# A masked attention kernel: mask adds moved from TensorE to GpSimd, and a reordered front

## What is computed

```python
h = jnp.maximum(_layernorm(x, axis=-1), 0.0)
neib_att = jnp.tanh(neigh @ Wn1 + bn1) @ Wn2 + bn2      # (4096, 32)
value = neigh @ Wv + bv                                  # (4096, 128)
x_att = jnp.tanh(h @ Wx1 + bx1) @ Wx2 + bx2              # (4096, 32)
ws = leaky_relu(x_att @ neib_att.T, 0.01)                # (4096, 4096)
ws = softmax(where(adj > 0, ws, NEG_BIG), axis=1)
out = x + concatenate([h @ Wfx + bfx, ws @ value], axis=1)
```

## Time and profile before

| what | value |
|---|---|
| median of 3 runs | 485.35 us (484.95 to 485.37) |
| the profiled execution | 485.15 us, its span 482.8 us |
| busy, share of the span | PE 96%, PEld 88%, DVE 89%, ACT 89%, POOL 54% |
| scores of step 0 start | 31.59 us |
| scores of step 11 start | 60.93 us |
| last scores start | 446.92 us |
| granted clock of TensorE, mean | 0.998 |

### The profile page before, as it was taken

How to read it: one execution, slowest core, us unless ns; L and a number is a source line. 1 busy time by engine, 2 the same in 40 slices (tenths; PEclk the granted TensorE clock), 3 DMA queues, 4 the chain that set the end, 5 groups by cost and what they waited for, 6 DMA issues and landing times.

```text
span 482.8 us, 10844 instructions
## 1 busy us (share of the span) xinstructions
PE 464.3 (96%) x3728; PEld 424.5 (88%) x3728; DVE 427.7 (89%) x820; ACT 428.3 (89%) x714; POOL 258.4 (54%) x361
## 2 busy tenths in 40 slices
PE   8997789999999999999999999999999999999997
PEld 7975579998899899998999899999899899999896
DVE  3678899999999899989999999989999899999764
ACT  2464899999999999999999999999999999999973
POOL 3108247853677547945686557845686455454300
PEclk9999999999999999999999999999999999999999
DMA  8944635457555655557456654657457554553000
GB/s 303 304 88 90 153 67 89 81 90 163 106 88 93 130 118 100 100 90 157 93 88 109 131 110 91 109 99 159 79 95 139 91 88 79 108 100 56 11 12 12
DMA packets 32373, 51.51 MB, mean 107 GB/s; under 512 B 2368, under 2 KB 22976, under 8 KB 32320
## 3 DMA queue, kind: packets, MB, share of 16 engines
q0 software_dynamic: 9216, 33.56, 42.5%
q1 hardware_dynamic: 22816, 17.17, 11.0%
q10 hardware_dynamic: 288, 0.10, 0.2%
HBM read 80.19 MB, written 4.19 MB: 175 GB/s over the span
## 4 chain that ended last, share of the span: by engine, by line
PE 75%; ACT 5%; issue 3%; DVE 3%; POOLq 0%; POOL 0%; DVEq 0%; ACTq 0%
PE ps_turned L922 20%; PE ps_product L943 11%; PE ps_product L945 11%; PE ps_product L944 11%; PE ps_scores L900 10%; PE ps_scores L899 6%; PE ps_product L865 3%; ACT scores L561 3%; ACT pt_hi L523 2%; DVE scores L706 2%; PE ps_product L857 1%; PE ps_product L841 1%; ACT scores L549 1%; PE ps_product L848 1%; PE ps_product L954 1%
## 5 line engine op out<-in xcount | busy, mean ns | idle before, releaser
L453 POOL TENSOR_TENSOR scores<-scores,mask 128x512 f32<-128x512 f32 x117 | 136.4, 1166 | 116.9 <-ACT scores L549 116.3
L688 DVE TENSOR_TENSOR pt_lo<-ps_turned,pt_hi 128x512 fp32r<-128x512 f32 x256 | 173.9, 685 | 20.8 <-PE ps_product L945 9.8
L523 ACT ACTIVATE pt_hi<-ps_turned 128x512 fp32r<-128x512 f32 x256 | 158.1, 618 | 20.9 <-PE ps_turned L922 20.3
L943 PE MATMUL ps_product<-pt_hi,v_hi 128*128 128x256 f32 x512 | 164.9, 322 | 0.1
L922 PE MATMUL ps_turned<-ident,scores 128*128 128x128 f32 x1024 | 153.8, 273 | 0.8 <-DVE pt_lo L688 0.6
L561 ACT ACTIVATE scores<-scores,low_top 128x1024 f32<-128x1024 f32 x128 | 151.5, 1183 | 0.0
L945 PE MATMUL ps_product<-pt_lo,v_hi 128*128 128x256 f32 x512 | 144.5, 282 | 0.0
L944 PE MATMUL ps_product<-pt_hi,v_lo 128*128 128x256 f32 x512 | 144.0, 281 | 0.0
L549 ACT ACTIVATE scores<-ps_scores 128x1024 f32<-128x1024 f32 x128 | 133.3, 1041 | 9.6 <-PE ps_scores L900 9.4
L922 PEld LDWEIGHTS ps_turned<-ident,scores 128*128 128x128 f32 x1024 | 121.9, 140 | 17.7 <-issue 2.0
L706 DVE CUSTOM_DVE_ANT_0 scores<-ps_scores,scores,low_top 128x1024 f32<-128x1024 f32 x96 | 122.5, 1276 | 0.9 <-ACT scores L549 0.4
(11 more groups left out here) (70 smaller groups left out, 359.8 us busy)
## 6 DMA issues: line engine op xcount, KB each, us to landing
adj_in<-in_adj POOLq DMA_DIRECT2D x60, 512.0 KB, 5.4
scores<-in_neigh_t SPq DMA_DIRECT2D x8, 512.0 KB, 7.9
x_rows<-in_x SPq DMA_DIRECT2D x7, 512.0 KB, 5.9
x_left<-in_x SPq DMA_DIRECT2D x8, 256.0 KB, 5.7
x_right<-in_x SPq DMA_DIRECT2D x16, 128.0 KB, 5.3
scores<-in_adj POOLq DMA_DIRECT2D x4, 512.0 KB, 6.4
out_h<-x_left SPq DMA_DIRECT2D x8, 256.0 KB, 2.3
out_h<-x_right SPq DMA_DIRECT2D x16, 128.0 KB, 2.1
```

The source lines that it names most:

```text
L453: pool.tensor_tensor(half, half, mask[:, s % MASK_RING, BANK:CHUNK], ALU.add).then_inc(masked, 1)
L523: act.activation(pt_hi[:, (2 * b + u) % HI_RING], pt[:, u], ACT.Copy).then_inc(hi_done, 1)
L688: dve.tensor_tensor(pt_lo[:, u], pt[:, u], pt_hi[:, (2 * b + u) % HI_RING].bitcast(FP32), ALU.subtract).then_inc(lo_done, 1)
L943: pe.matmul(product_of(g), v_hi[:, block, :], high, start=block == 0, stop=False)
```

## The change

In the loop, from step 11 on, TensorE writes the mask of the first 256 columns alone (QUARTER = 256), with one matmul, and the scores of the first half are made by two matmuls of 256 columns. GpSimd adds the mask to the other 768. ScalarE's relu comes first in its step. VectorE's `close` comes last ahead of the mask, and x work comes before the neighbour rest. In the front, the four loads into `adj_front` are issued together, the masks of chunks 4 to 11 are made in place by four operations over two chunks each and bypass the ring, warming transposes are left out, and x's first transposes come one neighbour step earlier. Several constants of the x schedule move.

```diff
 FRONT = 4 * LOAD
-TURN_X = 4
-FILL = (6, 6, 6, 4, 0, 0, 0, 0)
+TURN_X = 3
+FILL = (6, 0, 0, 0, 0, 0, 0, 0)
 EXP_LAG = CHUNKS + 1
...
-X_LOAD = -12
-X_STATS = (-6, -6, -6, -4)
+X_LOAD = -16
+X_STATS = (-7, -6, -5, -4)
 X_AGGR = -2
 X_RSTD = (-2, -2, -1, 0)
-X_NORM = (1, 3, 3, 4)
-X_TURN = (6, 8)
+X_NORM = (3, 4, 5, 5)
+X_TURN = (6, 7)
 X_FIRST, X_TANH = 10, 10
 X_SECOND = (14, 14)
 X_STACK = (14, 14)
-X_WIDE, X_LEFT = (15, 17, 19, 19), 19
-X_LEFT_LOAD, X_SUM = 8, (13, 18)
-X_RIGHT = 14
+X_WIDE, X_LEFT = (15, 18, 19, 19), 19
+X_LEFT_LOAD, X_SUM = 10, (13, 17)
+X_RIGHT = 7
 V_START, V_STRIDE = 2, 2
 LEFT_0 = 5
-AHEAD_STATS = 0
-WIDE_0 = 1
+AHEAD_STATS = -1
+WIDE_0 = 3
+FRONT_MASKS = (1, 2, 5, 7)
 V_FRONT, V_LAG = 4, 1
 POOL_MASKS = BACK_LAG
+QUARTER = BANK // 2
 WARM_UP = 15
...
         front_ready = [sem(f"front_ready{i}") for i in range(FRONT // LOAD)]
-        mask_done = sem("mask_done")
+        mask_done, front_masked = sem("mask_done"), sem("front_masked")
         scored = sem("scored")
...
             return b // ASTEPS + 2 if b >= 0 and b % ASTEPS == 0 and b // ASTEPS < AGROUPS - 2 else None
+        def ring_place(n):
+            return n - FRONT if n >= ADJ_RING else n
+        def made_in_front(n):
+            return ADJ_RING <= n < ADJ_RING + FRONT
+        def mask_of_chunk(n):
+            return adj_front[:, n - ADJ_RING, :] if made_in_front(n) else mask[:, ring_place(n) % MASK_RING, :]
...
             pool.wait_ge(rows_in[NEIGH_GROUPS - 1], 16)
-            load_adj(2 * LOAD)
-            pool.wait_ge(x_ahead_in, 16)
-            load_adj(3 * LOAD)
+            for p in range(FRONT // LOAD):
+                load_adj(ADJ_RING + p * LOAD)
             for i in range(NEWTON + 1):
                 rstd_of(1, i)
-            load_adj(4 * LOAD)
-            load_adj(5 * LOAD)
             for i in range(TILES):
...
                 if s % LOAD == 0 and n < STEPS and not ADJ_RING <= s < ADJ_RING + FRONT:
-                    pool.wait_ge(mask_done, s + LOAD)
+                    pool.wait_ge(mask_done, ring_place(s) + LOAD)
                     load_adj(n)
...
                     pool.wait_ge(risen, s + 1)
-                    half = scores[:, parity * TILES + tile, c * CHUNK + BANK:(c + 1) * CHUNK]
-                    pool.tensor_tensor(half, half, mask[:, s % MASK_RING, BANK:CHUNK], ALU.add).then_inc(masked, 1)
+                    rest = scores[:, parity * TILES + tile, c * CHUNK + QUARTER:(c + 1) * CHUNK]
+                    pool.tensor_tensor(rest, rest, mask_of_chunk(s)[:, QUARTER:CHUNK], ALU.add).then_inc(masked, 1)
                 for i in range(NEWTON + 1):
...
                 if s == GSTEPS:
-                    act.wait_ge(mask_done, ADJ_RING + FRONT)
+                    act.wait_ge(masked, ADJ_RING + FRONT - POOL_MASKS)
                 if s == (TILES - 1) * CHUNKS:
...
             def step(s):
+                rise(s)
                 hi(s, 0)
                 aggregate(s)
-                rise(s)
                 hi(s, 1)
...
-                k = n
-                if ADJ_RING <= n < ADJ_RING + FRONT:
-                    source = adj_front[:, n - ADJ_RING, :]
-                    dve.wait_ge(front_ready[(n - ADJ_RING) // LOAD], 16)
-                else:
-                    source = adj_in[:, n % ADJ_RING, :]
-                    dve.wait_ge(adj_ready[n % ADJ_RING // LOAD], 16 * ((n - FRONT if n >= ADJ_RING else n) // ADJ_RING + 1))
-                if n >= MASK_RING:
-                    dve.wait_ge(scored, n - MASK_RING + 1)
-                if n - MASK_RING >= POOL_MASKS:
-                    dve.wait_ge(masked, n - MASK_RING + 1 - POOL_MASKS)
-                dve.tensor_scalar(mask[:, n % MASK_RING, :], source, 0.0, MASKED, ALU.is_le,
+                if made_in_front(n):
+                    return
+                r = ring_place(n)
+                dve.wait_ge(adj_ready[r % ADJ_RING // LOAD], 16 * (r // ADJ_RING + 1))
+                if r >= MASK_RING:
+                    gone = r - MASK_RING
+                    if gone >= ADJ_RING:
+                        gone += FRONT
+                    dve.wait_ge(scored, gone + 1)
+                    if gone >= POOL_MASKS:
+                        dve.wait_ge(masked, gone + 1 - POOL_MASKS)
+                dve.tensor_scalar(mask[:, r % MASK_RING, :], adj_in[:, r % ADJ_RING, :], 0.0, MASKED, ALU.is_le,
                                   ALU.mult).then_inc(mask_done, 1)
+            def front_mask(p):
+                dve.wait_ge(front_ready[p], 16)
+                pair = adj_front[:, p * LOAD:(p + 1) * LOAD, :].rearrange("p a n -> p (a n)")
+                dve.tensor_scalar(pair, pair, 0.0, MASKED, ALU.is_le, ALU.mult).then_inc(front_masked, 1)
...
             def x_work(s):
+                for p in range(FRONT // LOAD):
+                    if s == FRONT_MASKS[p]:
+                        front_mask(p)
                 if s == AHEAD_STATS:
...
                 lo(s, 0)
+                x_work(s)
+                neigh_rest(s)
+                lo(s, 1)
                 close(s)
-                neigh_rest(s)
-                x_work(s)
-                lo(s, 1)
                 if POOL_MASKS <= s < STEPS - 2:
...
                 if h == 0:
-                    pe.wait_ge(mask_done, k + 1)
+                    if made_in_front(s):
+                        pe.wait_ge(front_masked, (s - ADJ_RING) // LOAD + 1)
+                    else:
+                        pe.wait_ge(mask_done, ring_place(s) + 1)
                     if s == 0:
...
                         pe.wait_ge(x_att, s // GSTEPS + 1)
-                half = slice(h * BANK, (h + 1) * BANK)
-                on_pool = h == 1 and s >= POOL_MASKS
-                if not on_pool:
-                    pe.matmul(ps[:, s % 2, half], ident_bf16, mask[:, s % MASK_RING, half], start=True, stop=False)
-                last = pe.matmul(ps[:, s % 2, half], xs[:, parity, tile * P:(tile + 1) * P],
-                                 neib[:, c * CHUNK + h * BANK:c * CHUNK + (h + 1) * BANK], start=on_pool, stop=True)
+                attention = xs[:, parity, tile * P:(tile + 1) * P]
+                def part(first, end, masked_here):
+                    cols = slice(first, end)
+                    if masked_here:
+                        pe.matmul(ps[:, s % 2, cols], ident_bf16, mask_of_chunk(s)[:, cols], start=True, stop=False)
+                    return pe.matmul(ps[:, s % 2, cols], attention, neib[:, c * CHUNK + first:c * CHUNK + end],
+                                     start=not masked_here, stop=True)
+                if s >= POOL_MASKS and h == 0:
+                    part(QUARTER, BANK, False)
+                    last = part(0, QUARTER, True)
+                else:
+                    last = part(h * BANK, (h + 1) * BANK, s < POOL_MASKS)
                 if h == 1:
```

## The result

The changed kernel takes 493.86 us (median of 4 runs, 490.58 to 495.50) where the kernel before takes 485.15: a ratio of 1.0173, with a 95% interval of 1.0139 to 1.0206. It is slower by 1.7%. The forecast was 472.6 us, with a range of 466 to 481.

What follows compares the result with a forecast made beforehand. TensorE was taken as the first bound, tied with ScalarE in plain steps. From 485.15 us, 10.8 for the loop and 1.3 and 0.4 for the front came off, giving 472.65, stated as 472.6, range 466 to 481.

Steps and rivals of the forecast that it cites:

- TensorE's split: Loop from step 11: narrower mask and score matmuls save 0.107 us a step over 101 steps, 10.8 us.
- GpSimd's longer add: Loop: adding 768 columns instead of 512 takes 1.59 us instead of 1.166, hidden, so no cost.
- relu first: ScalarE's step: the relu ahead of both copies delays VectorE's conversion and leaky pass enough to cover the longer add.
- front: Before the loop: 1.3 us from fewer warming transposes, 0.4 from the earlier x branch; steps 0 to 11 zero, 2 either side.
- constants and VectorE's order: Loop: moved x loads, stats and VectorE's close were costed at nothing.
- the longer add is therefore covered by the reordering: Plain step: the add ends 2.73 us after the relu's start, the leaky pass comes at 2.98, so no cost.
- crowd: GpSimd, steps 3 to 6: late adds cost about 0.5 us a group, cancelled by an equal gain on the exp chain.
- Rival 3: Loop: VectorE's conversion meets a running add in every step, 16 waits a group; slower, up to 491.5 us. Chance 0.08.
- The work of steps 3 to 5: GpSimd in each group: 11.4 us of work against 9.7 of time, so step 6's add can be 1 to 2 us late.
- the forecast 0.59: Plain step on TensorE: mask and score matmuls move the stream by 0.59 us instead of 0.69.
- Rival 1: Loop: ScalarE takes over and a group's eight plain steps gain nothing; 5.4 us instead of 10.8, so 478. Chance 0.20.
- TensorE stays busy: Front: with the warming transposes removed the granted clock stays at 1.00, so no loss there.

Runs made afterwards that it cites:

- e10: e3 with TensorE's split matmuls but GpSimd's old 512-column add, so columns 256 to 511 get no mask from step 11 on: 477.43 us.
- e3: Kernel before with only ScalarE's relu moved first in its step: 479.39 us, ratio 0.988.
- e11: e3 with GpSimd's 768-column add but TensorE's matmuls unchanged, so columns 256 to 511 are masked twice from step 11 on: 493.44 us.
- e5: Kernel before with the split (TensorE masks 256 columns, GpSimd adds 768) and the relu first; constants, VectorE's order and front unchanged: 492.78 us.
- e2: Kernel before with the split alone (GpSimd adds 768 columns, TensorE masks 256); order, constants and front unchanged: 506.53 us, ratio 1.044.
- e8: Kernel before with the changed front alone; loop, engine orders and x constants unchanged: 485.90 us, ratio 1.001.
- e17: e14 with WIDE_0 = 1 again, the wide layer back in step 1 instead of step 3: 477.51 us, ratio 0.985.
- e4: Changed kernel with the split undone: GpSimd adds 512 columns, TensorE masks 512; front, orders and constants stay: 487.39 us, ratio 1.003.
- e14: Kernel before with relu first and the new front, without the warming transposes; 512-column add, old constants: 479.88 us.
- e1: Changed kernel with x's normalisations put back early, X_NORM = (1, 3, 3, 4): 496.22 us, ratio 1.023.
- e7: Changed kernel with x's transposes one step later (steps 7 and 8) and the first stats at 10 instead of 9: 520.34 us, ratio 1.072.
- e6: e1 with GpSimd waiting, from step 11 on, before its sums and add until VectorE's next mask conversion is done: 485.10 us, ratio 0.9996.
- e13: Kernel before with relu first and the new front, but the warming transposes put back; 512-column add, old constants: 480.46 us.
- e15: Changed kernel with the warming transposes of before put back, FILL = (6, 6, 6, 4): 492.68 us.

## Why the prediction was wrong

Its steps against what the runs gave, in us of the whole kernel:

| step | predicted | measured |
|---|---|---|
| TensorE's split | -10.8 | -2.0 (e10 against e3) |
| GpSimd's longer add | 0 | +14.0 (e11 against e3), +15.4 (e5 against e10) |
| relu first | pays for the add | -5.7 (e3); the split costs +21.5 without it (e2), +13.4 with it (e5 against e3) |
| front | -1.7 | +0.8, within its interval (e8); -1.9 with WIDE_0 = 1 (e17 against e3) |
| constants and VectorE's order | 0 | +7.5 with 512-column adds (e4 against e14); +1.1 with 768, front included (changed kernel against e5) |

The rows don't add up, because the new constants and the longer add cost time in the same steps. One path goes e3, e10, e5, changed kernel: -5.7, -2.0, +15.4, +1.1. Another goes e14, e4, changed kernel: -5.4, +7.5, +6.5. Within 0.1 us both end at the measured +8.7.

**The step that failed** is "the longer add is therefore covered by the reordering", together with its crowd priced at 0.5 us a group. The cover was put at no cost, and the runs show +14.0 us for the add (e11). It was worked out for a plain step, and there it holds: most conversions still take 0.42 us. But the cost sits in steps that aren't plain. Steps 1 to 3 have a normalisation, a load, two sums and the add on GpSimd; the late add meets the next one, and the conversion is shut out over the whole string. Rival 3 had the place and the sign. Its form was wrong: it put one short wait into all 16 steps, where e1, e2, e5, e7 and e11 show one wait of 3.1 to 4.5 us in one step of a group. The 1.44 us of the earlier trace rows was shown for one add, and I took one instruction as the most that a conversion could lose. The Trainium skill's rule (SBUF — State Buffer, "Who interferes with whom") says that whoever issues first has the shared pair for the whole instruction and the other is blocked. I read it as one instruction against one, and e1 and e11 go beyond that by a factor of two to three. With the conversion of 0.41 us inside a normalisation (e3 at 251.04) the trace does not agree with the rule.

**A wait I did not look up, the second step that failed.** I costed each move of a constant against GpSimd's time, and not against who waits for the normalisations: `x_turn` in step 6. The moves, put at nothing, cost 7.5 us even with the short add (e4 against e14). The work of steps 3 to 5, which I had summed to 11.4 us in 9.7, was enough to see that the fourth normalisation could not be done by then. In the changed kernel this is the visible loss, 1.8 us a group; the longer add makes 1.1 of it (step 6 is 4.12 in e4) and the constants 0.7. e7 shows that moving the wait does not remove the loss.

**TensorE's 10.8 us.** The split shortens the scores: at 261.44 to 262.07 the chain of the changed kernel shows 0.64 us for them, and in other steps TensorE takes the forecast 0.59 from their start to the transposes, against 0.69. But in e10, with these shorter scores, the plain step is still 2.99, so ScalarE, which tied with TensorE there, holds it. Others stay at 3.2, since a relu that starts as soon as the scores end leaves the second copy waiting for the second transposes. Steps in which TensorE alone decides are few. With e10 the group goes from 52.85 to 52.67. Rival 1 priced this at half; a fifth was true.

**Relu first** was the change's real gain. I had seen it (20.3 us of copy waits) and used it up as cover instead of pricing it alone. In e3 it brings the group from 53.7 to 52.85.

**The front** was right in its first half (the scores of step 0 began at 30.46, about 1.1 us earlier), and wrong on the clock. I looked at the removed transposes, and argued that TensorE stays busy. It idled 0.69 us up to 8.3, after which the clock read 0.68, 0.66 and 0.66 in 7 to 12 us in e1, e4 and e6, and 1.00 in the other profiles of the same front. The larger hole was the wide layer's.

## What to carry to other kernels

Price a longer operation in the most crowded step of its engine, not in the plain one, and list who waits for everything that shares its queue. Where GpSimd's sums hold up a VectorE conversion, look at the longest string of sums without a gap, not the longest sum; a wait placed in that string lets the conversion in and made two kernels faster. A reorder and the load that it is meant to hide should be timed apart: here the one line of the reorder was worth more than the change.

## What the runs showed of the hardware

A mask conversion on VectorE, 0.42 us by itself, took 3.1 to 4.5 us when GpSimd ran its two-input sums back to back (e1, e2, e5, e7, e11), and got in at the end of the string: 0.30 us after it in e1. Between a sum and an add that followed without a gap it got no turn where the add's relu had ended 0.26 us or more before the sum did, and got one where that was 0.21 us or less (the changed kernel at 252.20). It ran in 0.41 us while GpSimd normalised (e3 at 251.04).

TensorE's granted clock fell to 0.50 in single windows of 1 us after an idle piece of 0.67 to 0.69 us near 8 us in e1, e4 and e6, and stayed at 1.00 after one of 0.67 to 0.74 us in the changed kernel, e7, e8, e14 and e17. A stop of about 3.1 us at 33 to 38 us stands in nine profiles. In seven the clock fell during it or up to 1.2 us behind it: it read 0.53 to 0.58 in 36 to 40 us in the changed kernel, e7, e13, e14 and e15, and 0.67 and 0.50 in 40 to 44 us in e4 and e6. In e1 and e8 it stayed at 1.00. In the loop it fell after stops of 1.9 to 2.9 us in e1, e2, e6, e7 and e11, and not after six of 1.8 to 2.6 us in e5.
